# Attention scores on halves of the TensorE array's rows, in a fused early-fusion transformer layer

## The reference

```python
NUM_HEADS = 12
q, k, v = (qkv[0], qkv[1], qkv[2])                           # B, 12 heads, 249 tokens, 16 wide
attn = jnp.einsum('bhnd,bhmd->bhnm', q, k) * Dh ** (-0.5)    # the scores
attn = fq_act(attn, s_attn)                                  # to 8-bit steps
attn = log_int_softmax(attn, s_attn)                         # shares as powers of two
o = jnp.einsum('bhnm,bhmd->bhnd', attn, v)
```

## Time and profile before

| what | value |
|---|---|
| median of three runs | 3520.66 us (3519.58 to 3520.66) |
| the profiled execution | 3518.62 us, span 3516.8 us |
| TensorE (PE) busy | 3381.6 us, 96% |
| VectorE (DVE) busy | 3368.5 us, 96% |
| ScalarE (ACT) busy | 3153.6 us, 90% |
| GpSimd (POOL) busy | 806.2 us, 23% |
| mean granted TensorE clock | 0.989 |

### The profile page before, as it was taken

How to read it: one execution, slowest core, us unless ns; L and a number is a source line. 1 busy time by engine, 2 the same in 40 slices (tenths; PEclk the granted TensorE clock), 3 DMA queues, 4 the chain that set the end, 5 groups by cost and what they waited for, 6 DMA issues and landing times.

```text
span 3516.8 us, 98077 instructions
## 1 busy us (share of the span) xinstructions
PE 3381.6 (96%) x30764; PEld 2898.6 (82%) x30764; DVE 3368.5 (96%) x10279; ACT 3153.6 (90%) x6228; POOL 806.2 (23%) x1647
## 2 busy tenths in 40 slices
PE   1589999999999999999999999999999999999999
PEld 1368888888888888888888888888888888888888
DVE  6699999999999999999999999999999999999995
ACT  2799999999999999999999999999999999999992
POOL 3222222222222222222221221222222222222210
PEclk9789999999999999999999999999999999999999
DMA  5101001000000000000000110100000000000000
GB/s 125 27 14 25 25 16 26 25 20 23 25 20 23 24 22 21 24 23 20 25 24 18 25 25 16 26 25 17 25 25 20 23 25 21 22 24 23 20 10 8
DMA packets 157123, 85.77 MB, mean 24 GB/s; under 512 B 51451, under 2 KB 154370, under 8 KB 156610
## 3 DMA queue, kind: packets, MB, share of 16 engines
q1 hardware_dynamic: 153692, 78.82, 9.0%
q10 hardware_dynamic: 2918, 0.67, 0.1%
HBM read 54.89 MB, written 12.24 MB: 19 GB/s over the span
## 4 chain that ended last, share of the span: by engine, by line
PE 92%; DVE 1%; issue 1%; ACT 0%; POOLq 0%; DVEq 0%; POOL 0%
PE pU L1183 33%; PE pY L1209 20%; PE pX L1075 5%; PE pX L1132 5%; PE pS L1120 4%; PE pS L1111 4%; PE pS L1121 4%; PE pX L1094 3%; PE pW L1195 3%; PE pO L1142 2%; PE pY L1192 1%; PE pX L1102 1%; PE pX L1088 1%; PE pX L1151 1%; PE pX L1082 1%
## 5 line engine op out<-in xcount | busy, mean ns | idle before, releaser
L1183 PE MATMUL pU<-x2T,UG 128*128 128x250 f16 x8704 | 1231.6, 270 | 1.0 <-ACT work L676 0.9
L1183 PEld LDWEIGHTS pU<-x2T,UG 128*128 128x128 f16 x8704 | 823.0, 97 | 108.7 <-ACT work L676 1.5
L1209 PE MATMUL pY<-WD,work 128*128 128x192 f32 (+1 forms) x4352 | 810.0, 328 | 0.0
L1209 PEld LDWEIGHTS pY<-WD,work 128*128 128x128 f32 (+1 forms) x4352 | 690.8, 187 | 3.9
L962 DVE SCALAR_TENSOR_TENSOR work<-work,cst 128x249 f32<-128x249 f32 (+1 forms) x1536 | 658.6, 484 | 8.4 <-issue 4.3
L623 ACT ACTIVATE work<-work,alpha 128x249 f32<-128x249 f32 (+1 forms) x1536 | 648.3, 509 | 15.2 <-DVE alpha L974 14.0
L607 ACT ACTIVATE work<-a,room 128x249 bf16<-128x249 int8 (+1 forms) x1536 | 648.3, 514 | 0.0
L1183 PE MATMUL pU<-x2T,UGB 67*128 67x250 f16 x2176 | 592.4, 272 | 0.0
L942 DVE TENSOR_REDUCE rmax<-a 128x4 f32<-128x996 int8 (+1 forms) x384 | 452.9, 1179 | 40.9 <-ACT a L598 40.9
L632 ACT ACTIVATE passing<-pX,cst 128x512 int16<-128x512 int16 (+3 forms) x768 | 480.8, 687 | 6.9 <-PE pX L1132 3.5
L598 ACT ACTIVATE a<-pS,cst 128x996 int8<-128x996 f32 (+1 forms) x384 | 421.4, 1097 | 70.3 <-PE pS L1111 70.1
(11 more groups left out here) (209 smaller groups left out, 5337.5 us busy)
## 6 DMA issues: line engine op xcount, KB each, us to landing
img<-in_x_dram SPq DMA_DIRECT2D x896, 23.5 KB
img<-in_x_dram SPq DMA_DIRECT2D x768, 21.4 KB
qz<-qb SPq DMA_DIRECT2D x768, 15.6 KB, 1.8
h<-in_txt_dram SPq DMA_DIRECT2D x64, 96.0 KB, 2.0
out_dram<-yout SPq DMA_DIRECT2D x64, 96.0 KB
out_dram<-yout SPq DMA_DIRECT2D x64, 90.8 KB
WD<-in_L_ffn_Wd_dram SPq DMA_DIRECT2D x1, 1536.0 KB, 7.6
work<-in_L_ffn_Wu_dram SPq DMA_DIRECT2D x2, 512.0 KB, 6.6
```

The source lines that it names most:

```text
L1183: a = mm(pU[:, s, q * EVEN:(q + 1) * EVEN], weights, x2T[i % 2][0:w, m, 0:EVEN], start=m == 0, stop=m == BLOCKS - 1)
L1209: a = mm(pY[0:n, t * 256:t * 256 + D], (act_[k % 2] if k else up[0])[:, c:c + n], WD[:, e, :], start=k == 0 and t == 0, stop=e == E - 1, s ...
```

## The change

The loop over the four heads of a score block goes 0, 2, 1, 3 instead of 0, 1, 2, 3, and each product takes only the half of the rows in which its head lies: rows 0 to 63 for heads 0 and 1, rows 64 to 127 for heads 2 and 3. The output places are the same, so each half writes to a bank of its own.

```diff
-                        for m in range(PER):
+                        for m in (0, 2, 1, 3):
+                            rows = slice(m // 2 * 2 * QUAD, (m // 2 + 1) * 2 * QUAD)
                             a = mm(pS[0:n, m // 2, (m % 2) * TOKENS:(m % 2 + 1) * TOKENS],
-                                   qz[:, g * PER + m, tcols[t]], kb[:, g, :], start=True, stop=True)
+                                   qz[rows, g * PER + m, tcols[t]], kb[rows, g, :], start=True, stop=True)
                         a.then_inc(s_ps, 1)
```

## The result

The changed kernel takes 3527.35 us (median of 15 runs) against 3520.26 for the kernel before (15 runs): ratio 1.0022, 95% interval 1.0014 to 1.0030, so 7 us slower with 5 to 11 allowed. The forecast was 3528. The profiled execution has a span of 3526.5 us against 3516.8. Its mean granted clock is 0.981 where the kernel before has 0.989, but that is not the difference: the kernel before was timed 24 times beside the first experiment, 10 times at 0.989 and 14 times at 0.981 to 0.983, with a median of 3519.6 us either way, and between 1000 and 2000 us the clock is 1.00 in both traces.

The account below looks back on a forecast made before the run. PE bounds one stretch of each image, VectorE the other; PE's grows by 0.008 - 0.07 + 0.078 + 0.108 = 0.124 us, times 62 images 7.7 us, on the median of 3520.66: 3528 us, range 3502 to 3560.

Parts of the forecast that it names:

- my own case: Halves overlap but switches eat the gain: 0.124 us more per image, 3528 us, range 3518 to 3537, chance 0.59.
- the f32 term: First f32 weight load of line 1209 after a score block loses its cover: 0.07 us each, bounds 0 to 0.09.
- the switch in: PE going from the whole array into row halves before a score block: 0.10 us.
- the stagger: Within a score block, the second half's product starts later than the first's: 0.01 us.
- late second half: Second half's 121-column weights might load behind the first half's: 0 to 0.04 us per such block, taken as 0.
- block 2: Image's second score block, 121 columns, before the value block, only one new switch: -0.07 us.
- Block 3: Image's third score block, text tokens, before f32 line 1209: +0.078 us.
- Block 4: Image's fourth score block, 121 columns, before f32 line 1209: +0.108 us.
- Block 1: Image's first score block, text tokens, before line 1183: +0.008 us.
- Two stretches: Per image VectorE sets the time from 1516.66 to 1527.23, PE the rest; PE gains there stop after 0.32 us.
- blocks 5 and 6: Last two score blocks, in VectorE's stretch: +0.008 and +0.076 us, hidden under PE's 0.20 us wait for line 668.
- cheap-switch rival: Switches to row halves cost little or nothing: 3501 us if free, capped by VectorE, 3505 at half price; chance 0.17.

Follow-up runs that it names:

- the first experiment: Changed kernel with the loop over heads back in the order 0, 1, 2, 3, halves kept: 3528.43 us, ratio 1.0024 to the kernel before.
- the run on one half: Changed kernel with all four products of a score block on rows 0 to 63: 3593.83 us, ratio 1.0211 to the kernel before.
- three moves: Changed kernel, two score blocks moved right behind value blocks and the experts' first up block behind transposes: 3507.38 us, ratio 0.9965 to the kernel before.

## Why the prediction was right

The mechanism came out as forecast: two rounds instead of four, a switch on each side that eats the gain, and a loss at the f32 weights. That 3528 met 3527.35 within 1 us is partly luck: the bounds of my own case were 3518 and 3537, and below the f32 term is too small while the switch in and the stagger are too large, so that the errors nearly cancel.

The sum is compared by starts. Besides that needs four more rows of the kernel before, from its PE timeline:

```profile
1509.92 0.38 PE L1195 MATMUL pW<-w3T,pick 96*128 96x250 bf16 x2
...
1510.57 1.47 PE L1209 MATMUL pY<-WD,work 128*128 128x192 f32 x8
...
1512.75 0.60 PE L1132 MATMUL pX<-ident,passing 121*128 121x121 bf16 x8
...
1513.62 1.47 PE L1209 MATMUL pY<-WD,work 128*128 128x192 f32 x8
```

**Streams.** Taken: two halves side by side, 0.212 us and 0.01 of stagger. Measured: 0.39 instead of 0.59 from first start to last end, and the run on one half gives the other bound. The second product starts at most 0.004 us after the first (a window of the PE timeline that ends at 1506.018 shows none of them, one that ends at 1506.022 shows two), so the 0.01 was too much.

**Switches.** Taken: 0.10 in, 0.11 out. In: from the start of line 1196 to the block it is 0.31 us (1505.71 to 1506.02) where two such products took 0.22 before (1509.92 to 1510.14): 0.09. Out: block to the next stage 0.32, of which two rounds are 0.21: 0.11. The Trainium skill ("TensorEngine Tiling (Array Packing)", Key Properties) says that a change of tiling mode drains the engine; for row halves the trace after agrees, with some 0.2 us of idle before the weight loads at five of the six blocks and again behind them.

**Weights without cover.** For 121 columns I took 0.03; blocks of 121 columns last 0.43 against 0.39: 0.04. The late second half did not come: the two halves' first loads go in together (0.19 us for all four). For f32 I took 0.07 of a possible 0.09: the eight f32 products behind blocks 3 and 4 last 1.57 against 1.47, so 0.10. This is the term that was furthest off, too small by 2 x 0.03 us per image. I had also put it in the wrong place: the block should have given way after 0.40 us before line 1209, and it does so after 0.32 and 0.35; the extra time lies inside the f32 products.

**Per block:** block 2 gives way after 0.36 instead of 0.52, and starts 0.09 later after its predecessor (1.45 against 1.36): -0.07 as forecast. Block 3: start 0.31 against 0.22, giving way after 0.32 against 0.43, f32 +0.10: +0.08 (0.078 forecast). Block 4: 0.54 against 0.44, 0.35 against 0.43, f32 +0.10: +0.12 (0.108). Block 1: +0.09 and -0.10, so -0.01 (0.008). That is 0.12 to 0.13 in rows rounded to 0.01, and 0.14 between the starts of two images, against 0.124 forecast.

**Two stretches.** The cut of the image into a stretch of VectorE and one of PE is what kept blocks 5 and 6 out of the sum. In the changed kernel, timeline of one image:

```profile
1521.69 0.56 DVE L937 TENSOR_TENSOR v<-pX,v_scale 128x384 int8<-128x384 f32 x1 [0.47 <-PE pX L1104]
...
1532.27 0.66 PE L1193 MATMUL pY<-BD,w3T 96*128 96x192 bf16 x6
```

From line 937 to the pick products it is 10.58 us; before it was 1527.23 - 1516.66 = 10.57. Nothing was added there, though both blocks in it pay switches.

**The rivals** fell by the trace: switches to halves aren't cheap (0.09 in, 0.11 out), and the halves overlap in full (0.39 against 0.60 on one half). The cheap-switch rival's cap, VectorE's 0.32 us, was approached but reached by no run: with three moves the image got 12 / 62 = 0.2 us shorter and the wait fell by about as much, to 0.09.

**What was wrong on the way:** the reason I gave for the alternation. The order of the heads doesn't matter (3528.43 against 3527.35 us); only the halves do. The Trainium skill ("TensorE: Matmul & The Clock Gate", Part 3, The mechanism) has products start in strict program order and weight loads overlap a running product only in another row group. By strict order, 0, 1, 2, 3 would take three rounds; it took two. And the four loads of a block, two of them for a half whose first product is still running, are over in 0.12 us. The measurement decides.

## What to carry to other kernels

Splitting the array for a small contraction saves half of the stream, but here each change of the array's shape cost about 0.1 us, one into the halves and one out of them, and the first weights behind it cost extra (0.04 us for 121 bf16 columns, 0.10 for f32 of 128). Four products with a stream of 249 win no more than that (0.21 us); so try to put blocks of different tiled shapes side by side and not in front of f32 weights, look at what waits for the stages that the moved block now stands in front of, and time the moved order on whole rows beside it. And ask first, stretch by stretch, which engine sets the time: here the same edit was worth -4, +13 and 0 us by where it stood.

## What the runs showed that I had not expected

Products on the other half of the rows overtake: with the order 0, 1, 2, 3 the block has two rounds and 0.39 us, as with 0, 2, 1, 3, while all four on one half take 0.60. And f32 products straight behind a switch cost about 0.10 us extra, more than twice the 0.04 of 121 bf16 columns. Both halves in the same bank were not tried.
